# Two-layer shifted-window attention on one core: order of the output path, normalisation sums in pairs, masking on GpSimd, and start and end of the pipeline rearranged

## What is computed

```python
xw = windows(roll(_gn(x), (-4, -4)))            # 4 windows of 64 tokens per image
q, k, v = xw @ Wq.T, xw @ Wk.T, xw @ Wv.T + bv  # 16 heads of 16 channels
qn, kn = q / max(|q|, 1e-12), k / max(|k|, 1e-12)
logits = (qn @ kn.T) * exp(min(logit_scale, log 100))
logits += 16 * sigmoid(table[rel_position])     # table: a small MLP of coordinates
logits = where(mask, -inf, logits)              # windows that the roll cut
z = softmax(logits) @ v @ Wo.T + bo
x = x + roll(back(z), (4, 4))
```

## Time and profile before

| | us |
|---|---|
| median of 2 runs (763.71 and 770.17) | 766.94 |
| the profiled execution, time of the launch | 770.32 |
| its span, first to last instruction | 768.5 |
| TensorE matmuls busy | 728.5 (95%) |
| GpSimd busy | 553.6 (72%) |
| VectorE, ScalarE busy | 503.5, 498.5 |

### The profile page before, as it was taken

One profiled execution on the slowest core, in us unless ns is written; L12 is line 12 of the kernel. 1 busy time (PEld: TensorE's weight loads), 2 busy tenths in 40 slices (PEclk: granted clock), 3 DMA queues, 4 the chain that ended last, 5 costly groups with the idle time before them and its releaser, 6 DMA issues.

```text
span 768.5 us, 38488 instructions
## 1 busy us (share of the span) xinstructions
PE 728.5 (95%) x15518; PEld 652.5 (85%) x15518; DVE 503.5 (66%) x1177; ACT 498.5 (65%) x848; POOL 553.6 (72%) x913
## 2 busy tenths in 40 slices
PE   3689899999999999999999999999999999999995
PEld 3578788888888889898989888888888888888984
DVE  4545466666666666667777667677766767776642
ACT  4556467676677667676777676666667666666650
POOL 4475668777877787788888777877777787777660
PEclk9789899999999999999999999999999999999995
DMA  4666200000000000000000000000000000000000
GB/s 116 156 157 172 65 0 0 0 1 0 0 0 0 0 0 0 0 0 0 1 0 0 28 28 14 27 27 25 16 27 27 14 27 27 27 14 27 29 31 32
DMA packets 14041, 21.45 MB, mean 28 GB/s; under 512 B 3756, under 2 KB 5045, under 8 KB 14005
## 3 DMA queue, kind: packets, MB, share of 16 engines
q1 hardware_dynamic: 13461, 20.23, 8.8%
q10 hardware_dynamic: 544, 0.79, 0.3%
HBM read 12.60 MB, written 8.42 MB: 27 GB/s over the span
## 4 chain that ended last, share of the span: by engine, by line
PE 89%; issue 3%; DVE 3%; DMA 2%; DVEq 1%; ACT 0%; SPq 0%; ACTq 0%
PE ps_qk L380 24%; PE ps_mix L496 17%; PE ps_qk L508 14%; PE ps_mix L414 9%; PE ps_score L404 7%; PE ps_score L469 6%; PE ps_mix L419 4%; PE ps_mix L392 4%; PE ps_mix L486 3%; DVE x_out L794 2%; DMA bias_rev<-table_scratch 1%; PE ps_score L433 1%; DMA table_scratch<-table 1%; DMA cpb<-in_L_cpb 0%; DVE exp_bias L737 0%
## 5 line engine op out<-in xcount | busy, mean ns | idle before, releaser
L963 POOL TENSOR_TENSOR probs<-probs,exp_bias 128x512 f32<-128x512 f32 x256 | 326.0, 1305 | 18.9 <-ACT probs L643 18.9
L380 PE MATMUL ps_qk<-w_qk,xn 128*128 128x512 f32 x768 | 200.0, 410 | 0.0
L643 ACT ACTIVATE probs<-ps_score,lower 128x1024 f32<-128x1024 f32 x128 | 135.7, 1111 | 66.8 <-PE ps_score L469 66.8
L380 PEld LDWEIGHTS ps_qk<-w_qk,xn 128*128 128x128 f32 x768 | 144.0, 194 | 30.2
L496 PE MATMUL ps_mix<-v_ones,probs 64*64 64x17 f32 x8064 | 133.4, 209 | 3.4 <-issue 3.4
L574 ACT ACTIVATE squares<-ps_qk 128x512 f32<-128x512 f32 x128 | 77.0, 602 | 87.1 <-PE ps_qk L380 87.1
L758 DVE TENSOR_REDUCE sums_sq<-squares 128x32 f32<-128x512 f32 x128 | 87.2, 682 | 68.9 <-ACT squares L574 68.8
L496 PEld LDWEIGHTS ps_mix<-v_ones,probs 64*64 64x64 f32 x8064 | 126.8, 136 | 5.5 <-issue 3.7
L783 DVE SCALAR_TENSOR_TENSOR unit<-root,ps_qk 128x512 f32<-128x512 f32 x128 | 82.4, 683 | 58.9 <-POOL root L953 58.9
L508 PE MATMUL ps_qk<-w_v,xn 128*128 128x256 f32 x768 | 113.9, 300 | 5.4 <-DVE unit L783 4.6
L508 PEld LDWEIGHTS ps_qk<-w_v,xn 128*128 128x128 f32 x768 | 100.2, 198 | 7.7 <-issue 6.0
(11 more groups left out here) (73 smaller groups left out, 867.8 us busy)
## 6 DMA issues: line engine op xcount, KB each, us to landing
x_all<-in_x SPq DMA_DIRECT2D x32, 256.0 KB, 3.1
out<-x_out SPq DMA_DIRECT2D x32, 256.0 KB, 2.1
bias_rev<-table_scratch SPq DMA_DIRECT2D x4, 452.0 KB
w_qk_in<-in_L_matrices ACTq DMA_DIRECT2D x1, 512.0 KB, 4.6
w_o_in<-in_L_matrices SPq DMA_DIRECT2D x4, 128.0 KB
w_qk_in<-in_L_matrices SPq DMA_DIRECT2D x1, 512.0 KB, 5.5
w_v_in<-in_L_matrices ACTq DMA_DIRECT2D x1, 256.0 KB, 4.9
w_v_in<-in_L_matrices SPq DMA_DIRECT2D x1, 256.0 KB, 6.2
```

Of the source, the lines that this page charges most:

```text
L380: last = nc.tensor.matmul(ps_qk[:, e, :], xn[:, px, t.parity, c, e * P:(e + 1) * P], w_qk[:, pw, c, :], start=(c == 0 and i == 0), stop=(c ...
L643: nc.scalar.activation(probs[:, t.parity, 2 * i:2 * i + 2, :, :, :, :].rearrange("p r e c a n -> p r (e c a n)"), ps_score[:, 2 * i:2 * i ...
L963: nc.gpsimd.tensor_tensor(pr, pr, exp_bias[:, t.layer, r, :, :, :, :].rearrange("p e c a n -> p (e c a n)"), ALU.mult).then_inc(weighted, 1)
```

## The change

- TensorE issues `turn_back` between the two halves of `project_qk`; ScalarE's high part (L588) and VectorE's `keep_rest` move forward with it, ahead of the second half's steps.
- The projected output lies in two banks, half c in bank c of `ps_mix`. `project_out` does half 0 whole and then half 1, waits for the rest after the first four matmuls, and signals each half; `add_residual` waits for each half alone.
- `mix` drops two of its four waits, and its wide first matmul (L486) becomes a matmul of 32 rows and one column that only clears; the small ones are 128.
- `sum_groups`, `group_variance` and the root of the group variance are done for two images at once, every second iteration; moments are taken four jobs ahead (`AHEAD`).
- `exp` is four instructions of 512 columns.
- The first layer's bias is masked by GpSimd in iteration 1, after `newton`; the table is computed per layer. DMAs at the start are in another order; the SP queue waits in iteration 4 until job 5 has its unit vectors before it loads more of `x`.
- Dummy matmuls (`keep_busy`) run in TensorE's idle times before and in iteration 0.
- TensorE's loop covers jobs 4 to 63 (before: to 61). The rest after job 63 is a `drain` of its own in which the last three jobs use three pairs of banks and are interleaved; VectorE takes half of the last job's `weigh`; the last image is stored in two halves, and the flag is computed beside that.

The core of the diff:

```diff
+        def multiply_bias(engine, l, e, c):
+            ...
+            engine.tensor_tensor(exp_bias[...], heads..., seen..., ALU.mult).then_inc(bias_ready, 1)
+        def home_of(t, last):
+            return (ps_mix, ps_qk, ps_score)[last]
...
             def project_out(t, last=0):
...
                 for c in range(CC):
                     for a in range(2):
                         for part in range(2):
-                            nc.tensor.matmul(z_cols[:, c, :], ..., mixed[:, 0, a, :], start=(c + a + part == 0), ...)
-                pe.wait_ge(mixed_ready, t.count(1, 1))
-                for c in range(CC):
+                            nc.tensor.matmul(home[:, c, 0:TOKENS], ..., kept[:, 0, a, :], start=(a + part == 0), ...)
+                    if c == 0:
+                        pe.wait_ge(mixed_ready, t.count(1, 1))
                     for a in range(2):
-                        last = nc.tensor.matmul(z_cols[:, c, :], ..., mixed[:, 1, a, :], ...)
-                last.then_inc(z_done, 1)
+                        done = nc.tensor.matmul(home[:, c, 0:TOKENS], ..., kept[:, 1, a, :], ...)
+                    done.then_inc(z_done, 1)
...
-                past(pe, x_updated, t.count(2, 0))
-                past(pe, mixed_ready, t.count(1, 0))
-                pe.wait_ge(v_ready, t.count(1, 1))
-                pe.wait_ge(weighted, t.count(4, 4))
-                nc.tensor.matmul(mix_cols[:, 0, 0, :], probs[0:N, ...], v_ones[0:N, ...], ...)
+                if last == 0:
+                    past(pe, x_updated, t.count(2, 0))
+                    pe.wait_ge(weighted, t.count(4, 4 - 2 * t.exact))
+                    nc.tensor.matmul(ps_mix[0:N, 0, 511:512], ident[0:32, 0:N], ident[0:32, 0:1], ...)
...
-                sum_groups(j, base, job(j, base, 2))
+                if j != 0:
+                    sum_groups(j, base)          # even j only, both images of the pair
+                if j == -1 and not base.exact:
+                    keep_busy(9)
                 project_qk(now, 0)
+                turn_back(oldest)
                 project_qk(now, 1)
-                turn_back(oldest)
+                if j == 0:
+                    sum_groups(j, base)
+                    ...
+                        begin_table(1); keep_busy(12); end_table(1)
                 turn(before)
                 project_out(oldest)
...
+            def drain(base):                     # TensorE
+                now, before, older = (job(JOBS - 1, base, -k) for k in range(3))
+                turn(now)
+                turn_back(older)
+                score(now)
+                project_out(older)
+                mix(before, 1)
+                mix(now, 2, (0,))
+                turn_back(before, 1)
+                mix(now, 2, (1,))
+                project_out(before, 1)
+                turn_back(now, 2)
+                sum_lost()
+                project_out(now, 2)
...
-            both_passes(pe, iteration, ((4, JOBS - 2),))
+            both_passes(pe, iteration, drain, ((4, JOBS),))
...
+                if j == 4 and not base.exact:    # SP
+                    sp.wait_ge(unit_ready, 2 * 6)
...
+                if j == 1 and not base.exact:    # GpSimd, after newton(1)
+                    pool.wait_ge(masks_in, 2 * 16)
+                    pool.wait_ge(bias_in, 2 * 16)
+                    for e in range(2):
+                        for c in range(CC):
+                            multiply_bias(nc.gpsimd, 0, e, c)
```

More of the change, by code:

```diff
@@ L69, in count, with pairs @@
         return 2 * per_image * self.half + (per_image * self.parity + done)
+    def pairs(self, per_pair, done):
+        return per_pair * self.half + done
     def count_exact(self, per_image, done):
@@ L75, in moves @@
     def moves(self, step):
-        return step * self.half
+        return step * (self.half - self.exact * self.parity)
     @property
@@ L209, in past, with run @@
                 engine.wait_ge(semaphore, value)
-        def run(engine, iteration, exact, loops):
+        def run(engine, iteration, drain, exact, loops):
             def some(a, b):
@@ L231, in both_passes @@
             with engine.If(again != 0):
-                run(engine, iteration, 1, loops)
+                run(engine, iteration, drain, 1, loops)
         def job(j, base, k):
@@ L599, in log_sums @@
             def log_sums(j, base):
-                t, u = job(j, base, 0), job(j, base, 2)
+                t, u = job(j, base, 0), pair(j, base)
                 if t is None and u is None:
@@ L605, in log_sums @@
                 if u is not None:
-                    act.wait_ge(gn_step, u.count(4, 4))
-                past(act, seeded, chain(base, 1, 0))
+                    act.wait_ge(gn_step, u.pairs(4, 4))
+                past(act, seeded, chain(j, base, 1, 0))
                 at = root_columns(t, u)
@@ L694, in iteration, with drain @@
                     if base.exact:
-                        act.wait_ge(z_done, JOBS)
+                        act.wait_ge(z_done, 2 * JOBS)
                     round_weights(0, 2)
-            both_passes(act, iteration)
+            def drain(base):
+                now, before, older = (job(JOBS - 1, base, -k) for k in range(3))
+                keep_q(now, 0)
+                keep_q(now, 1)
+                keep_mixed(older)
+                keep_shift(now)
+                for r in range(GROUPS):
+                    exp(now, r)
+                keep_mixed(before, 1)
+                keep_mixed(now, 2)
+            both_passes(act, iteration, drain)
         @block.vector
@@ L885, in iteration @@
                 divide(older)
-                if j == 0 and not base.exact:
-                    for e in range(2):
-                        for c in range(CC):
-                            mask_bias(0, e, c)
+                if j == 0:
+                    moments(ahead)
                 if IMAGES - 4 <= j < IMAGES and not base.exact:
@@ L893, in iteration, with drain @@
                     split_weights(0, base.exact, 2)
-                    if not base.exact:
-                        add_out_bias()
-                if j == JOBS + 1 and not base.exact:
-                    find_lost()
+            def drain(base):
+                now, before, older = (job(JOBS - 1, base, -k) for k in range(3))
+                keep_k(now)
+                refine_shift(now)
+                cap(now)
+                keep_rest(older)
+                for r in (1, 3):
+                    dve.wait_ge(exped, now.count(4, r + 1))
+                    multiply_probs(nc.vector, now, r, last_weighted)
+                divide(before, 1)
+                for c in range(CC):
+                    add_residual(older, c)
+                keep_rest(before, 1)
+                divide(now, 2)
+                if not base.exact:
+                    find_lost()
+                for c in range(CC):
+                    add_residual(before, c, 1)
+                keep_rest(now, 2)
+                if not base.exact:
+                    dve.wait_ge(flag_summed, 1)
+                    nc.vector.tensor_copy(flag[:, :], ps_mix[0:1, 1, 0:1]).then_inc(flag_ready, 1)
+                for c in range(CC):
+                    add_residual(now, c, 2)
             def find_lost():
```

450 lines of the change are left out of this document (270 added, 180 removed).

## The result

The changed kernel takes 710.33 us (708.90 and 711.75), the kernel before 766.94: a ratio of 0.926, 95% interval 0.908 to 0.945.

The account below looks back on a forecast made before the run. TensorE was taken to bound the kernel. Loop -19.9, start -3.7, iterations 3 to 6 -5.5 and end -8.0 sum to -37.1 us; 770.3 becomes 733.2, less 3.4 for the median about 730 us, range 715 to 746.

Parts of the forecast that it names:

- iterations 3 to 6: Four early iterations after the start: 48.5 us instead of 53.97, -5.5 us, keeping 5.5 of the 9.5 us lost there.
- Turn back earlier: Loop, between the q/k halves: same 0.44 us on TensorE, no gain itself; avoids a stall of up to 0.5 us per image.
- Two banks: Loop, output projection: second residual sum ends before the scores, so the mix waits less; 0.15 us per image.
- The narrow matmul: Loop, start of the mix: clearing matmul costs 0.20 us with extra records; gain 0.12 per image, bounds -0.10 and +0.29.
- Two waits fewer: Loop, start of the mix: dropping two waits from the first instruction was counted at nothing.
- The paired sums: Loop, group sums of two images together: 0.115 us less per image; sign, q/k starts 10.6 and 10.85 us apart in turn.
- bound for the best case: Loop: lowest time per image, 10.60 us, if all the loop's edits came at their best.
- The start: Up to iteration 3's q/k projection: 50.3 instead of 54.01 us, -3.7, with first q/k at 13.8 and maskings 2.1 each.
- The end: After the last v projection: 19.9 us instead of 27.9, -8.0, by three pairs of banks and interleaved last jobs.
- Rival 1: Loop, before the mix: none of the wait goes, the loop gives only 6.5 us, 743 us in all; chance 0.11.
- rival 2: Start: gaps and low clock stay, GpSimd's maskings take 4 us apiece, 743 us; chance 0.08, including the joint case.
- Rival 3: TensorE's loop body falls out of its instruction store, 2.4 us lost per image, 864 us; chance 0.01.

Follow-up runs that it names:

- E4: The kernel before with only turn back moved between the halves of the q/k projection, with the two output copies: 759.3 us, ratio 0.989.
- E3: The changed kernel with the projected output in one bank again, signalled once at the end, turn back still early: 730.4 us, ratio 0.949.
- E12: The changed kernel with the two dropped waits of the mix put back: 720.9 us, ratio 0.937.
- E6: The changed kernel without the SP queue's wait in iteration 4: 714.0 us, ratio 0.927.
- E9: The control, the changed kernel itself run once more beside other runs: 714.0 us, ratio 0.926.
- E2: The changed kernel with turn back again behind both halves of the q/k projection, with the two output copies: 743.8 us, ratio 0.966.
- E7: The changed kernel with no dummy matmuls: 718.6 us, ratio 0.932.
- E8: The changed kernel with VectorE doing two of the first layer's four maskings and the second layer's maskings in iterations 28, 29, 30 and 32: 710.0 us, ratio 0.922.
- E11: The changed kernel with both edits of E8, and VectorE also doing two of job 0's four products: 710.2 us, ratio 0.925.

## Why the prediction was wrong

*The bound.* Right: TensorE bounds the loop before and after, and the unit vectors are never late in it. The loop got 0.74 us per image shorter over the stretch where 0.36 was forecast. That is 21.5 us, the whole error: the start came 1.9 us worse than forecast, iterations 3 to 6 2.2 better, the end 0.3 worse, and these three cancel.

*Turn back earlier.* Here the step failed: "it costs TensorE the same 0.44 us in another place; after transposes a 256-column group runs at its normal rate (1.10 for eight, as 1.62 for twelve)". I took the rate of v's projection for that of the output's. The other four matmuls of the same group took 0.47 in the row below, which is 0.94 for eight. The difference was a wait for ScalarE's copy (E4). So turn back had a gain of its own, 0.15, and I had it at nothing.

*Two banks.* Right in kind: the second sum ends before the scores. I sized it at 0.15 as if it stood alone. It is what makes the clearing matmul free: undoing it costs 0.24 to 0.34 (E3).

*The narrow matmul.* Taken as 0.20 us with the extra records, bounds from nothing to 0.39 and the extra records. It is at the lower end: 0.00 to 0.06 on the chain, and 0.06 for the extra records. The row nearest to it, which I named, was a score record at 0.018 us, and I left it for a surcharge for a change of tile shape whose size no row showed.

*Two waits fewer.* "I count at nothing": 0.10 to 0.13 (E12).

*The paired sums.* 0.115 forecast, 0.12 + 0.11 every second image measured. The sign that I gave for it, starts of q/k at 10.6 and 10.85 us in turn, was wrong by my own rows: the 0.12 lies ahead of the start of a q/k projection and the 0.11 behind it, so each of the two intervals holds one of them. They are about 10.31 and 10.35 us in turn.

Together, from first score to end of mix, 0.27 was forecast and 0.50 came, and in the projection 0.19 instead of nothing. 0.115 + 0.19 + 0.50 = 0.81, which is 11.15 - 10.34. My bound for the best case, 10.60 per image, assumed that each edit is paid by itself; that is why the range was too high as well. (Added up from its own terms, 0.115 + 0.15 + 0.29 off 11.11, it would have been 10.56.)

*The start.* -1.8 us instead of -3.7. GpSimd's maskings cost 1.5 us each and not 2.1, but they began at 34.0 and not 31.3. The first q/k projection runs at 15.65, not 13.8: the first group sums need the moments of both images and come at 8.18, in the kernel before at 6.03. It takes 3.25 us for the 2.9 that I took. These two are 2.2 of the 2.7 us. The v projection of iteration 2 ran in part at the lower clock (2.47 us for 1.61, mean granted clock 0.62). Iterations 3 to 6 lose 5.0 us against the new period, where I had kept 5.5: 2.2 in the two gaps, and most of the rest in projections at a lower clock, as v at 73.68 (2.41 us for 1.61, granted clock 0.60) and the half of q/k behind it (2.14 for 1.40). The reason I gave for keeping fewer, the x traffic, is not the cause (E6).

*The end.* -7.7 us, forecast -8.0, and from the last v projection 20.7 us, forecast 19.9. That this came so close is in part luck, since the end alone took 33.3 us in the control (E9) and 30.9 here. Interleaving took the serial chain of job 62 off the path.

*Rivals.* Rival 1 is out. Of rival 2 the masking at 4 us is out; gaps do stay, two at the start. Rival 3 didn't come: TensorE is busy 579.51 of 580.51 us, and from 88 to 690 us no packet moves on its instruction queue. The Trainium skill, "Runtime: NRT & Kernel Launch", section "Instruction fetch mechanics", has instructions arrive in blocks that are fetched while the one before runs, mostly hidden. Packets of 0.02 MB on TensorE's instruction queue, one in each of the windows 54.5 to 55.5, 60.5 to 61.5, 70 to 70.5, 73 to 74, 83 to 83.5 and 86.5 to 87 us, agree that blocks are fetched. As for hidden, a gap follows two of these six (71.06 and 84.69); in the kernel before a gap follows four of the eight packets of the first 104 us. So where the code is met for the first time here, up to half of the fetches are not hidden, if they are what makes the gaps; no run removed them to show that.

## What to carry to other kernels

When an engine is busy 99% of the time, look inside the runs: divide each group's time by its count, and compare it with the rate of the same kind of matmul one row further down before comparing with another group. A short instruction at a change of stage is free only if every wait in front of it is met, and worked off, while the stage before still runs; so an earlier producer, a cheaper instruction and fewer waits are to be priced together, not as a sum. An "issue" on a chain is not yet idle time: the engine's timeline tells. And an edit that only moves work can be the condition of the next one (E2), so undoing one edit gives more than it gains alone.

## What the runs showed that I had not expected

- Two waits already met, in front of one matmul, cost (with the computing of their counts) 0.10 to 0.13 us per image (E12).
- Gaps of about 1 us inside TensorE's runs come in the first pass through its code with 8 GB/s of other traffic as with 168 (E6). Removing dummy matmuls brought another one (E7), and one at the end came and went between executions of the same TensorE program (1.50 us in E8, 0.67 in E9, none in E11).
- The column of the granted clock says 1.00 in 15 to 21 us of E7, while twelve q/k matmuls take 4.70 us there against 2.8 to 2.9 in the loop. The 4.70 is near what twelve take where the column shows a lower clock (4.58 us at 95.15 in the kernel before, mean granted clock 0.61). So at the very start I go by durations, not by the column.
